# Channel maxima and means from one PSUM bank for two groups of positions

## The reference, cut to what matters

```
def _zpool(x):
    return jnp.concatenate([x.max(axis=1, keepdims=True), x.mean(axis=1, keepdims=True)], axis=1)

def _gate(x, w, g, b, m, v):
    z = _zpool(x)
    y = lax.conv_general_dilated(z, w, (1, 1), [(3, 3), (3, 3)], dimension_numbers=('NCHW', 'OIHW', 'NCHW'))
    scale = g / jnp.sqrt(v + EPS)
    y = (y - m[None, :, None, None]) * scale[None, :, None, None] + b[None, :, None, None]
    return x * jax.nn.sigmoid(y)
b1 = _gate(x.transpose(0, 2, 1, 3), ...)    # pools over H
b2 = _gate(x.transpose(0, 3, 2, 1), ...)    # pools over W
b3 = _gate(x, w_hw, ...)                    # pools over the channels
...
return (wts * branches).sum(axis=1)
```

## Time and profile before

| what | value |
|---|---|
| median of 3 runs | 2962.48 us (2961.73 to 2963.66) |
| the profiled execution | 2961.15 us, of which the span is 2959.0 us |
| TensorE busy | 80% of the span |
| VectorE busy | 77% |
| ScalarE busy | 58% |
| POOL busy | 47% |
| mean granted TensorE clock | 0.937 of full speed |

### The profile page before, as it was taken

The page is one execution under the profiler, slowest core; times in us unless marked ns, Lnnn a source line. Parts: engine busy times, 40 slices in busy tenths (PEclk is TensorE's granted clock), DMA queues, the critical chain, the costliest instruction groups (busy, mean ns, idle before and its releaser), DMA issues.

```text
span 2959.0 us, 68446 instructions
## 1 busy us (share of the span) xinstructions
PE 2369.5 (80%) x27236; PEld 1319.3 (45%) x27236; DVE 2293.1 (77%) x4555; ACT 1707.6 (58%) x4440; POOL 1383.2 (47%) x1052
## 2 busy tenths in 40 slices
PE   0157728899698978899798978898898979898776
PEld 0132315544454545444454545444544545454443
DVE  6868675878787887878887887888887888886443
ACT  0231118655766558654875567654876567655776
POOL 4304471365724574455634573356534572364222
PEclk9977859999899989999899989999999989999998
DMA  5400040004110240005100330005010421011101
GB/s 157 118 3 10 34 149 16 30 30 150 60 37 23 80 143 30 30 30 167 49 31 23 116 107 31 30 30 186 31 44 21 139 72 45 23 51 58 44 30 37
DMA packets 91347, 184.51 MB, mean 62 GB/s; under 512 B 37510, under 2 KB 50454, under 8 KB 80406
## 3 DMA queue, kind: packets, MB, share of 16 engines
q1 hardware_dynamic: 88854, 177.78, 18.5%
q10 hardware_dynamic: 2176, 2.36, 0.3%
HBM read 107.23 MB, written 72.86 MB: 61 GB/s over the span
## 4 chain that ended last, share of the span: by engine, by line
PE 52%; DVE 22%; ACT 11%; issue 7%; POOL 5%; ACTq 1%; SPq 0%; DMA 0%; DVEq 0%; POOLq 0%
PE F L1950 21%; PE QP L2006 6%; PE QP L2022 4%; PE QP L2013 4%; PE SP L2038 3%; PE O L2066 2%; ACT xs L1129 2%; PE PTR L2048 2%; PE F L1828 2%; PE F L1852 1%; ACT g_raw L1011 1%; DVE Z L1630 1%; DVE xs L1748 1%; ACT tmp L968 1%; ACTq L927 1%
## 5 line engine op out<-in xcount | busy, mean ns | idle before, releaser
L1950 PE MATMUL F<-g_raw,cw_hi 128*128 128x512 f16 x2304 | 701.6, 387 | 35.9 <-ACT tmp L1000 23.3
L856 POOL TENSOR_TENSOR xs<-xs,rec 128x512 f32<-128x512 f32 x256 | 283.2, 1107 | 754.2 <-DVE rec L1740 752.3
L1129 ACT ACTIVATE xs<-xs,mx 128x64 f32<-128x64 f32 x2048 | 511.3, 336 | 89.0 <-DVE mx L1735 88.9
L1950 PE MATMUL F<-g_raw,cw_lo 128*128 128x512 f16 x1152 | 443.9, 385 | 0.0
L1950 PEld LDWEIGHTS F<-g_raw,cw_hi 128*128 128x128 f16 x2304 | 220.8, 99 | 293.9 <-ACT tmp L1000 26.9
L1724 DVE TENSOR_TENSOR xs<-SP,bias 128x512 f32<-128x512 f32 (+2 forms) x384 | 181.6, 500 | 112.4 <-PE SP L2038 111.2
L841 POOL TENSOR_TENSOR tmp<-X,uw 128x512 f32<-128x512 f32 x128 | 175.6, 1384 | 186.2 <-DVE X L1587 172.2
L2006 PE MATMUL QP<-tok_hi,qkv_hi 128*128 128x512 f16 x512 | 199.1, 389 | 75.8 <-ACT qq L1114 24.1
L1739 DVE TENSOR_REDUCE sums<-xs 128x8 f32<-128x512 f32 x256 | 173.5, 678 | 94.9 <-ACT xs L1129 93.9
L1852 PE MATMUL F<-ident,g_raw 128*128 128x128 f32 x512 | 102.7, 318 | 156.1 <-ACT tmp L968 143.4
L1327 DVE SCALAR_TENSOR_TENSOR g_raw<-l0c,gn,g_raw 128x512 f16<-128x512 f32 x192 | 177.1, 967 | 52.2 <-ACT g_raw L990 36.3
(11 more groups left out here) (288 smaller groups left out, 5652.1 us busy)
## 6 DMA issues: line engine op xcount, KB each, us to landing
X<-in_x SPq DMA_DIRECT2D x32, 1024.0 KB, 6.2
scratch_x<-X SPq DMA_DIRECT2D x32, 1024.0 KB, 5.2
xs<-scratch_x SPq DMA_DIRECT2D x56, 512.0 KB, 3.6
out_x<-xs SPq DMA_DIRECT2D x56, 512.0 KB, 2.7
l0c<-scratch_t SPq DMA_DIRECT2D x8, 1876.0 KB, 10.5
l0c<-in_c_ind SPq DMA_DIRECT2D x8, 1024.0 KB, 6.3
l0c<-scratch_t SPq DMA_DIRECT2D x8, 640.0 KB, 12.7
l0c<-scratch_t SPq DMA_DIRECT2D x8, 576.0 KB, 13.2
```

The source lines that it names most:

```text
L856: G.tensor_tensor(keyed(sc[:, u % 4, :]), keyed(sc[:, u % 4, :]), rec[:, u % 4, :].unsqueeze(2).to_broadcast([P, 8, TOK]), ALU.mult).then_ ...
L1129: last = S.activation(keys, keys, ACT.Exp, bias=mx[:, u % 4, i:i + 1])
L1950: last = T.matmul(F[:, n % 2, :], wgt[:, ci, C3 * comp + dx, P * co:P * co + P], win[which], start=(ci == 0 and dx == 0 and j == 0), stop= ...
```

## The change

Group j now lies in bank i mod 2, where i = j // 2 is the step, in columns 256 (j mod 2) and on, so a step's two groups fill one whole bank. f_tr and f_max count steps instead of groups (16 an image). VectorE takes both groups' maxima with one instruction over a view of 2 x 256 columns. ScalarE still takes one mean a group, but both wait for the step's one maximum instruction. TensorE waits once a step, for the maxima and the means of step i-2; before, it waited for each group on those of group j-2.

```diff
--- before.py
+++ after.py
@@ -334,8 +334,8 @@
         v_raw = sem("v_raw", 1)
         x_dve = sem("x_dve", 4)
         g_ready = sem("g_ready", 8)
-        f_tr = sem("f_tr", 32)
-        f_max = sem("f_max", 32)
+        f_tr = sem("f_tr", 16)
+        f_max = sem("f_max", 16)
         z_ready = sem("z_ready", 1)
         y_done = sem("y_done", 1)
         y_copied = sem("y_copied", 1)
@@ -961,11 +961,11 @@
 
                     def channel_means(i):
 
+                        act.wait_ge(f_max, at(f_max, i + 1))
                         for j in range(2 * i, 2 * i + 2):
-                            act.wait_ge(f_max, at(f_max, j + 1))
                             if j >= 2:
                                 act.wait_ge(f_sum, at(f_sum, j - 1))
-                            S.activation(tmp[:, j % 2, 0:C], F[:, j % 2, 0:C], ACT.Copy, scale=1.0 / C,
+                            S.activation(tmp[:, j % 2, 0:C], F[:, i % 2, C * (j % 2):C * (j % 2) + C], ACT.Copy, scale=1.0 / C,
                                          accum_out=Z3[:, 1, 2 + j:3 + j]).then_inc(f_sum, 1)
 
                     def pad_waves():
@@ -1427,9 +1427,9 @@
                         dve.wait_ge(pads_zero, 2)
                     for i in range(PAIRS // 2):
 
-                        for j in range(2 * i, 2 * i + 2):
-                            dve.wait_ge(f_tr, at(f_tr, j + 1))
-                            V.tensor_reduce(Z3[:, 0, 2 + j:3 + j], F[:, j % 2, 0:C], AX.X, ALU.max).then_inc(f_max, 1)
+                        dve.wait_ge(f_tr, at(f_tr, i + 1))
+                        V.tensor_reduce(Z3[:, 0, 2 + 2 * i:4 + 2 * i], F[:, i % 2, :].rearrange("p (j c) -> p j c", j=2),
+                                        AX.X, ALU.max).then_inc(f_max, 1)
                         yield f"reduce{i}"
                     dve.wait_ge(gn_coef, at(gn_coef, 1))
                     seq.link(V.tensor_scalar(r64[:, :], g_r, 1.0 / W, None, ALU.mult))
@@ -1843,14 +1843,15 @@
                         for j in range(2 * i, 2 * i + 2):
                             if j % (PAIRS // 4) == 0:
                                 pe.wait_ge(g_ready, at(g_ready, CT * (j // (PAIRS // 4) + 1)))
-                            if j >= 2:
-                                pe.wait_ge(f_max, at(f_max, j - 1))
-                                pe.wait_ge(f_sum, at(f_sum, j - 1))
-                            else:
+                            if i < 2:
                                 pe.wait_ge(gn_coef, at(gn_coef, 1))
+                            elif j % 2 == 0:
+                                pe.wait_ge(f_max, at(f_max, i - 1))
+                                pe.wait_ge(f_sum, at(f_sum, 2 * i - 2))
                             for t in range(CT):
-                                last = T.transpose(F[:, j % 2, P * t:P * t + P], Gn[:, t, P * j:P * j + P], ident[:, :])
-                            last.then_inc(f_tr, 1)
+                                last = T.transpose(F[:, i % 2, C * (j % 2) + P * t:C * (j % 2) + P * t + P],
+                                                   Gn[:, t, P * j:P * j + P], ident[:, :])
+                        last.then_inc(f_tr, 1)
                         yield f"reduce{i}"
                     yield "zpool"
 
@@ -1858,7 +1859,7 @@
                         pe.wait_ge(l0c_in, 64 * img)
                     else:
                         pe.wait_ge(bands_in, 48)
-                    pe.wait_ge(f_max, at(f_max, PAIRS))
+                    pe.wait_ge(f_max, at(f_max, PAIRS // 2))
                     pe.wait_ge(f_sum, at(f_sum, PAIRS))
                     for i in range(2 * DJ):
                         ch, dj = divmod(i, DJ)
```

## The result

The changed kernel takes 2970.5 us (median of 20 runs, 2962.41 to 2979.19) where the kernel before takes 2961.86 (20 runs, 2958.14 to 2971.88). The ratio is 1.0024, with a 95% interval of 1.0014 to 1.0034: slower by 0.24%, 8.6 us. The forecast was 2956.2 in a range of 2949 to 2964.

A forecast was written before the change was run, and what follows sets the result against it. TensorE carried 52% of the chain; ScalarE, 89% busy, limited the stages of images 2 to 7. Terms -5.8 - 1.0 + 0.6 = -6.2 us on 2961.15 gave 2954.95, or 2956.2 as a median; range 2949 to 2964.

The forecast's parts named there:

- Image 0: Image 0's stage: the loosened loop lets L1252 start at 153.4 instead of 159.20; -5.8 us, bounds -6.4 and 0.
- VectorE waits for POOL as foreseen: End of image 0's stage: scaling the pooled rows waits for POOL's row sums, ending at 152.13, which the edit doesn't speed.
- The loop covers two steps: Image 0's last five steps: 2.74 us for two steps, 1.37 us a step in place of 1.78.
- Image 1: Image 1's stage: step 7 no longer waits for the mean of step 6; -1.0 us, between +0.5 and -3.
- Images 2 to 7: Stages of these images: ScalarE's list sets the length; +0.1 us an image, +0.6 for six, bounds -1.5 and +0.9 an image.
- The step: The prediction's reckoning for images 2 to 7: mean 0 comes 0.55 us later, ScalarE's list stays the same, +0.1 us an image.
- rival 4: Images 2 to 7: TensorE's waits gather into longer idle pieces and its clock falls; 2.1 us an image, 2969; chance 0.11.
- TensorE's 3.38 us wait for L968: Image 5's stage, at 1787.24: the wait was to vanish without gain, since ScalarE has the same list to do.
- The argument that held it down: Against rival 4: TensorE has no more work nor time than before, and its longest idle piece, 3.38 us, gets shorter.
- a chain of engines without an anchor in absolute time: What follows in image 0: the forecast's reason for carrying its -5.8 us on to the total.
- its unknown: Whole images: the same 3400 matmuls took 331.0 or 327.6 us, so shifted starts can move an image by some 3 us.
- the section named in the prediction: "A second HAM failure mode: psum-queue depth-cycling": clock oscillation where TensorE idles briefly between groups while cycling through banks; cited under rival 4.

The follow-up runs named there:

- the seven placements of the old scheme: The kernel before, and the same with one, two, three, four or six hidden VectorE fills in image 0 or one in image 7: 2961.9 to 2979.9 us.

## Why the prediction was wrong

**Image 0: right.** The end of its stage in the profile after:

```profile
142.19 1.94 PE L1852 MATMUL F<-ident,g_raw 128*128 128x128 f32 x8 [0.89 <-ACT tmp L968]
...
143.31 0.69 DVE L1431 TENSOR_REDUCE Z<-F 128x2 f32<-128x512 f32 x1 [1.29 <-PE F L1852]
...
145.88 4.45 PE L1866 MATMUL F<-Z,l0c 128*128 128x32 f32 x20 [1.75 <-ACT tmp L968]
...
152.00 0.29 POOL L905 TENSOR_TENSOR Z<-tmp 128x64 f32<-128x64 f32 x1
...
152.39 0.35 DVE L1439 TENSOR_SCALAR Z<-Z,gn 128x128 f32<-128x128 f32 x1 [3.05 <-POOL Z L905]
...
153.43 0.41 DVE L1252 TENSOR_TENSOR qq<-tok 128x256 f32<-128x256 f32 x1
```

L1866 starts at 145.88 (forecast 145.7), VectorE waits for POOL as foreseen, and L1252 starts at 153.43 where 153.4 was forecast: -5.77 us for a term of -5.8. The loop covers two steps, x8 transposes between waits, at 421 ns a transpose in both kernels.

**Image 1: right in the stage.** Up to the start of L1866 it is 0.9 us shorter in this profile and 1.3 on average, for a term of -1.0. The image as a whole gives this back: 327.5 against 327.3 us on average.

**Images 2 to 7: here it failed.** The term was +0.1 us an image, with bounds of -1.5 and +0.9. Measured is +2.1 an image, and +3.8 for the last with what follows it. The step reckoned what ScalarE's list costs and found that it stays the same, which the rows bear out: mean 0 comes 0.5 us later after the first transpose of image 5 (forecast 0.55), and the stage lasts 46.3 us for 46.1. It priced nothing for what TensorE's regrouped idle time does to TensorE's clock. That was rival 4: waits gathered into longer pieces, more time at the lower level (it took half as much again; measured in the stage is a rise from 7.4 to 12.0 us), 2.1 us an image and 2969 in all. It had a chance of 0.11. The step also let TensorE's 3.38 us wait for L968 vanish, and 2.81 us of it remained. From rival 4 only the place differs: scores, transposes and output products are hit more than a projection. The argument that held it down was: no more idle time than before, and a longest piece that gets shorter. The second is true (3.38 to 2.81 us), the first nearly (in the first 46 us of images 2 to 7 TensorE idles 10.2 us on average in the old scheme and 10.6 in the new), and neither decides: low stretches stand behind the pieces of 1.8 to 2.2 us earlier in the stage, where there had been pieces of up to 1.0 and no low stretch. The row for it stood in the profile: in the earlier trace rows the clock of image 5's stage was 0.91, and the forecast never asked ahead of which instruction.

Rival 4's price was met in part by luck. It was worked out inside the stage alone; 1.25 of the 2.1 us come behind it, in untouched code, where the clock falls or not with the moment at which TensorE comes to a thin piece of work.

**The sum: its form was wrong.** It carried image 0's gain to the end because what follows is "a chain of engines without an anchor in absolute time". With the old scheme in images 1 to 7 and the gain in image 0 the kernel took 2966.7, slower than before by 6.7. By these rows the granted clock acts like such an anchor: an image of the old scheme mostly lasts 327.6 or 331.0 us, by where the clock falls. The prediction named this as its unknown, 3 us an image, and then left it out of the range, which took in only the bounds of the terms. Fills that nobody waits for moved the total by 2 to 18 us, and the seven placements of the old scheme span 18 us, more than the forecast's whole range of 15. The kernel before is also the fastest of its seven placements, so the comparison started from a favourable one.

The Trainium skill's page "TensorE: Matmul & The Clock Gate", section "What's actually happening", says that how many matmuls of one kernel run at the low clock differs from run to run. Here single runs of one kernel spread over 14 us (before) and 17 us (changed), and the medians of the old scheme over 18 us from edit to edit: the kernel before gave the same six image lengths twice, while the changed one gave other lengths in its second profile (326.0, 331.0, 331.1, 329.2, 329.6, 329.2) and the same median. With the oscillation that the same page describes for short idle pieces between groups (the section named in the prediction) the trace agrees where the clock of 0.68 stands behind the 2.13 us wait; the 0.50 behind the 24 thin matmuls is another case, for TensorE was not idle there.

**What stays open.** That the regrouped idle time is the cause rests on rows (the waits of 1.8 to 2.2 us and the clock behind them) and on the separation of the two schemes' clocks, not on a kernel with the new scheme and the old pieces of idle time; that one was not made. A direct cost, perhaps the later first maximum of each step, may have a share: with doubled transposes it comes to some 0.5 us a stage by one pair of profiles, and without them none shows. Nor do these runs tell why the code behind the stage, which has the same instructions, loses 1.25 us an image. It isn't settled either why a hidden fill in image 0 leads to one length of image rather than the other: the kernel with its fill in image 7 alone reached image 1 at 445.5 us, the kernel before at 442.9 and 443.6, with the same instructions up to there. Most kernels were profiled in one execution, and single executions of the kernel before differ by up to 14 us, so a length of one image in one profile is not yet that of the kernel. No kernel that was run beats the one before.

## What to carry to other kernels

Looser handshakes can let an engine run ahead, so that its short waits flow together into long ones; on TensorE look at the instruction behind the longest new wait and at the granted clock there before the gain is counted. When a kernel's repeated stages come in two lengths with the same instructions (here 327.6 and 331.0 us), its time is partly a matter of placement: a difference of a few tenths of a per cent between two builds is then no verdict on the edit, and both versions should be timed with a few harmless shifts. A gain early in such a kernel is worth what its image is shorter by only on average over placements.

## What was not expected of the hardware

One VectorE fill of 0.48 us, with 2.38 us of waiting left behind it, made the kernel 18 us (0.61%) longer, repeatably (six runs, 2975.1 to 2987.3). The clock can fall in a stretch in which TensorE counts as busy: during 24 matmuls of one column it fell in one kernel (3.40 us for them, the window behind at 0.50) and not in the other (2.84 us, 1.00), and the 64 score products took 1.99 and 1.16 us. The view's clock of 1.00 can mean that nothing was recorded: image 0's transposes took 421 ns under it, later ones 273. Two back-to-back maxima of 128x256 and one of 128x512 cost nearly the same, 0.75 and 0.69 us.
